# A causal attention layer with routed experts: queries and keys as two fp32r parts of 48 rows a head, two heads side by side in the rows of TensorE's array

## What is computed

```python
h = _layernorm(x, axis=-1) * (1 + ca) + sa
qkv = jnp.einsum('bsd,ed->bse', h, w_qkv) + b_qkv          # 16 heads of 16
scores = jnp.einsum('bhqd,bhkd->bhqk', q, k) / math.sqrt(Hd)
attn = jax.nn.softmax(scores + causal[None, None], axis=-1)
out = jnp.einsum('bhqk,bhkd->bhqd', attn, v)
x = x + ga * (jnp.einsum('bsd,ed->bse', out, w_out) + b_out)
h = _layernorm(x, axis=-1) * (1 + cb) + sb
x = x + gb * _L0_ffn_ref(h, ...)       # top-1 routing, 8 experts, gelu
```

## Time and profile before

| | us |
|---|---|
| median of 3 timed runs (785.0 to 790.39) | 787.31 |
| span of the profiled execution, first to last instruction | 782.6 |
| PE busy, share of the span | 689.1, 88% |
| DVE busy | 561.1, 72% |
| ACT busy | 459.5, 59% |
| POOL busy | 133.9, 17% |

### The profile page before, as it was taken

The page is one execution under the profiler, slowest core; times in us unless marked ns, Lnnn a source line. Parts: engine busy times, 40 slices in busy tenths (PEclk is TensorE's granted clock), DMA queues, the critical chain, the costliest instruction groups (busy, mean ns, idle before and its releaser), DMA issues.

```text
span 782.6 us, 12208 instructions
## 1 busy us (share of the span) xinstructions
PE 689.1 (88%) x4290; PEld 367.2 (47%) x4290; DVE 561.1 (72%) x1467; ACT 459.5 (59%) x962; POOL 133.9 (17%) x194
## 2 busy tenths in 40 slices
PE   4686989999999998999999999989996279999994
PEld 3564534432323343323332323242543269999994
DVE  7754778788888787988888898960435437777762
ACT  1422445566676667766677676657783336656551
POOL 6000222220001132003310201100105300121122
PEclk9869889999999999999999999999999559999998
DMA  7436126630006033005900006000004283455200
GB/s 243 109 76 144 41 57 147 162 68 14 2 0 162 1 81 81 2 1 124 308 1 1 1 1 214 1 28 1 28 28 162 90 234 115 155 182 201 92 23 17
DMA packets 42111, 66.53 MB, mean 85 GB/s; under 512 B 3822, under 2 KB 31985, under 8 KB 41466
## 3 DMA queue, kind: packets, MB, share of 16 engines
q1 hardware_dynamic: 39746, 59.44, 27.3%
q0 software_dynamic: 2304, 6.31, 2.2%
HBM read 39.36 MB, written 26.78 MB: 85 GB/s over the span
## 4 chain that ended last, share of the span: by engine, by line
PE 74%; DVE 10%; ACT 8%; issue 4%; DMA 2%; POOL 1%; SPq 0%; DVEq 0%; POOLq 0%; ACTq 0%
PE bank L1245 17%; PE bank L1295 15%; PE bank L1325 14%; PE bank L1430 9%; PE bank L1413 8%; ACT probs L802 4%; PE bank L1187 3%; DVE chunk_max L1049 2%; PE bank L1350 2%; PE bank L1216 1%; PE bank L1396 1%; ACT qk_sb L751 1%; PE bank L1373 1%; PE bank L1228 1%; DVE stats L907 1%
## 5 line engine op out<-in xcount | busy, mean ns | idle before, releaser
L802 ACT ACTIVATE probs<-bank 128x512 f32<-128x512 f32 (+3 forms) x640 | 298.3, 537 | 124.1 <-PE bank L1325 123.0
L1049 DVE TENSOR_REDUCE chunk_max<-bank 128x1 f32<-128x512 f32 x384 | 250.7, 685 | 36.9 <-PE bank L1295 35.9
L1325 PE MATMUL bank<-stacks 104*128 104x512 bf16 (+3 forms) x640 | 195.4, 356 | 13.5 <-ACT probs L802 10.1
L1295 PE MATMUL bank<-stacks 96*128 96x512 bf16 (+3 forms) x640 | 197.7, 359 | 7.9 <-DVE chunk_max L1049 3.2
L1245 PE MATMUL bank<-probs,v_sb 128*32 128x512 f32 (+3 forms) x1280 | 151.6, 546 | 0.1
L1055 DVE CUSTOM_DVE_ANT_0 masked<-bank,causal 128x128 bf16<-128x128 f32 (+3 forms) x256 | 120.7, 484 | 15.4 <-PE bank L1295 14.6
L1295 PEld LDWEIGHTS bank<-stacks 96*128 96x128 bf16 x640 | 56.0, 98 | 160.0 <-DVE chunk_max L1049 79.4
L698 POOL TENSOR_SCALAR_AFFINE_SELECT probs<-probs 128x512 f32<-128x512 f32 x64 | 40.6, 635 | 397.4 <-ACT probs L802 397.4
L1325 PEld LDWEIGHTS bank<-stacks 104*128 104x128 bf16 x640 | 62.2, 100 | 98.7 <-ACT probs L802 65.6
L1430 PE MATMUL bank<-w_split,acts 128*128 128x256 f32 x576 | 79.9, 284 | 0.0
L1430 PEld LDWEIGHTS bank<-w_split,acts 128*128 128x128 f32 x576 | 74.5, 190 | 1.5 <-issue 0.8
(11 more groups left out here) (140 smaller groups left out, 533.6 us busy)
## 6 DMA issues: line engine op xcount, KB each, us to landing
stacks<-qk_rows SPq DMA_DIRECT2D x6, 1536.0 KB, 12.4
w_raw<-w_in SPq DMA_DIRECT2D x8, 1024.0 KB, 5.0
w_raw<-w_down SPq DMA_DIRECT2D x8, 1024.0 KB, 8.0
qk_rows<-part SPq DMA_DIRECT2D x32, 192.0 KB, 2.9
slot_rows<-empty SPq DMA_DIRECT2D x1, 5140.0 KB, 28.9
slots_sb<-slot_rows SPq DMA_DIRECT2D x8, 514.0 KB, 4.0
qk_rows<-part SPq DMA_DIRECT2D x32, 128.0 KB, 2.4
stacks<-qk_rows SPq DMA_DIRECT2D x8, 384.0 KB, 4.5
```

The lines of the kernel that those rows point to most:

```text
L802: act.activation(probs[:, s % 3, h, 0:width], bank[SCORE_BANKS[u % 3]][:, 0:width], ACT.Exp)\
L1049: dve.tensor_reduce(to, src[:, 0:QB], AX.X, ALU.max).then_inc(max_read, 1)
L1295: pe.matmul(bank[MAX_BANKS[u % 3]][:, 0:width], stack(g, 0)[0:KR, h, q0:q0 + P], stack(g, 1)[0:KR, h, c * QB:c * QB + width], start=True, ...
L1325: pe.matmul(bank[SCORE_BANKS[u % 3]][:, 0:QB - lo], stack(g, 1)[0:KR + MR, h, kt * P:(kt + 1) * P], stack(g, 0)[0:KR + MR, h, b * QB + lo: ...
```

## The change

Queries and keys are split in two parts of type fp32r, three products, 48 rows a head. A head's stack then fits in half of the array's 128 rows: heads 0 and 1 of a group lie in rows 0 to 51, heads 2 and 3 in rows 64 to 115 (48 rows, and 4 for the maxima). The order of units within a query tile and of the heads in a step is such that neighbours in the list of max units, or of scores, come from different halves.

- ScalarE's second cast, one of two subtractions and the third part go; a store writes two parts in 4 DMAs instead of 6, a load reads in 4 DMAs (two halves, two sides) instead of 2. The bytes of a stack load are the same (half the rows, twice the width of a number).
- The maxima's rows no longer go to the stacks by ScalarE and VectorE: ScalarE copies the turned rows to `row_sb` (after.py L811), and SP sends them with two DMAs to both halves (L632). The ones go by eight DMAs out of `row_sb` (L599). `max_part` is fp32, and its transposes are fp32.
- SP now follows the plan: stores, loads (`load`), rows (`max_rows`), weights (`experts`) stand in one order. The fill of `slot_rows` follows group 3's load at once, as before.
- The planner's rates are others (a matmul at 3.4 columns a ns instead of 2.4, rows placed 3500 ns after their transposes instead of 1700), and the plan comes out differently.
- The values are kept 18 columns a head apart; a weigh matmul still loads 32.

```diff
-PARTS_Q = [0, 0, 0, 1, 1, 2]
-PARTS_K = [0, 1, 2, 0, 1, 0]
-KR = HD * len(PARTS_Q)
-MR = 2 * HG
+PAIRS = HG // 2
+HEADS = (0, 2, 1, 3)
+HALF = P // 2
+PARTS_Q = [0, 0, 1]
+PARTS_K = [1, 0, 0]
+NR = len(PARTS_Q)
+KR = HD * NR
+MR = 2 * PAIRS
...
-    return [[(qt, h, c) for qt in range(TB) for h in range(HG) for c in range(b + 1)] for b in range(NB)]
+    return [[(qt, 2 * a + p, c) for qt in range(TB) for p in range(PAIRS) for c in range(b + 1) for a in range(2)]
+            for b in range(NB)]
...
-TENSOR_RATE, VECTOR_RATE, SCALAR_RATE = 2.4, 0.96, 1.2
-VECTOR_FIXED, SCALAR_FIXED, MASK_TIME = 75, 60, 700
+TENSOR_RATE, VECTOR_RATE, SCALAR_RATE = 3.4, 0.96, 1.2
+VECTOR_FIXED, SCALAR_FIXED, MASK_TIME = 68, 50, 700
...
-            tensor(300, formed)
-            placed_at[n] = now + 1700
-            vector[-1] = max(vector[-1], now + 550) + 450
+            tensor(500, formed)
+            placed_at[n] = now + 3500
...
-        stacks = sb1("stacks", [P, 2, 2, HG, S], BF16)
+        stacks = sb1("stacks", [P, 2, 2, PAIRS, S], F32R)
...
+        def stack(g, side, h, rows):
+
+            return stacks[HALF * (h // 2):HALF * (h // 2) + rows, g % 2, side, h % 2, :]
...
+                if ev[0] == "load":
+                    g = ev[1]
+                    sp.wait_ge(parts_stored, 16 * STORES * NB * (g + 1))
+                    if g >= 2:
+
+                        sp.wait_ge(scored, HG * (last_step[(g - 1) * NB - 1] + 1))
+                    load_stacks(g, slice(0, S), stacked[g])
+                    if g == NG - 1:
+                        sp.wait_ge(empty_ready, 1)
+                        sp.dma_start(slot_rows.rearrange("(t p) d -> p t d", p=P),
...
+                if ev[0] == "max_rows":
+
+                    n = ev[1]
+                    g, b = divmod(n, NB)
+                    sp.wait_ge(misc_read_a, misc_reads(misc_use[ev])[0] + 1)
+                    for a in range(2):
+                        sp.dma_start(stacks[HALF * a + KR:HALF * a + KR + MR, g % 2, 0, :, b * QB:(b + 1) * QB]
+                                     .bitcast(F32),
+                                     row_sb[MR * a:MR * (a + 1), n % 2, :].bitcast(F32).rearrange("p (h s) -> p h s", h=1)
+                                     .broadcast_to([MR, PAIRS, QB])).then_inc(max_rows[n % 2], 16)
...
+        def low_part(eng, n, done):
+
+            eng.wait_ge(high_ready, n + 1)
+            eng.tensor_tensor(part[:, 1, :], qk_sb[:, :], part[:, 0, :].bitcast(F32), ALU.subtract).then_inc(done, 1)
...
-                if ev[0] == "split":
-                    second_part(ev[1], ev[2])
...
-                    rows = stack(g, 0)[KR:KR + MR, :, b * QB:(b + 1) * QB]
-                    dve.wait_ge(max_row0, n + 1)
-                    dve.tensor_copy(rows[:, 1:HG, :], rows[:, 0:1, :].broadcast_to([MR, HG - 1, QB]))\
-                        .then_inc(max_rows, 1)
...
-                    pe.matmul(bank[SCORE_BANKS[u % 3]][:, 0:QB - lo], stack(g, 1)[0:KR + MR, h, kt * P:(kt + 1) * P],
-                              stack(g, 0)[0:KR + MR, h, b * QB + lo:(b + 1) * QB], start=True, stop=True)\
+                    pe.matmul(bank[SCORE_BANKS[u % 3]][:, 0:QB - lo], stack(g, 1, head, KR + MR)[:, kt * P:(kt + 1) * P],
+                              stack(g, 0, head, KR + MR)[:, b * QB + lo:(b + 1) * QB], start=True, stop=True)\
```

More of the change, by code:

```diff
@@ L214, in project @@
                 parts_at[split[0]] = now + SPLIT_TIME
+        if loads and not split and loads[0] in parts_at and loads[0] - 2 in scored_at \
+                and now >= scored_at[loads[0] - 2] + 1000:
+            plan.append(("load", loads.pop(0)))
     weigh = None
```

241 lines of the change are left out of this document (118 added, 123 removed).

## The result

The changed kernel takes **947.7 us** (median of 4 runs, 946.79 to 949.98) against 788.17 of the kernel before (4 runs, 785.0 to 790.39): a ratio of 1.2035, with a 95% interval of 1.2001 to 1.2069. It was forecast at 759. The profiled execution spans 946.2 us (before 782.6), and its mean granted clock is 0.787 (before 0.943).

A forecast was written before the change was run, and what follows sets the result against it. PE was taken to bound the attention, VectorE next. Terms -41 + 15 + 5 - 7 + 2 - 2 = -28 us gave a span of 754.6 instead of 782.6, 759 us with the median's 4.7; range 715 to 794.

The forecast's parts named there:

- What bounds the kernel: Attention: PE bounds both its stages, at a granted clock of 0.98 in the first; VectorE is the next bound.
- stage B: The attention's two passes together, 80 to 510 us; PE busy 408.5 of 430 us, VectorE 367.3.
- the last sentence: Closing signs of being wrong, among them a fall of the granted clock in the attention's passes, with PE busy less.
- Part 1: Max and scores matmuls in the attention's passes: overlapping halves bring 0.179 down to 0.1435 us each, 41 us less.
- the 0.118 taken for them: Pace in us for a max or scores matmul following one in the other half, read from the experts' fp32r matmuls.
- Part 2: Scores moved ahead of the last max unit: 16 us less in the later stage, 16 more in the passes, 0.
- Parts 3 and 4: Maxima's rows sent by SP: later landing at blocks 0 to 3, 11, 15, +15; queue behind group 3's load, +5.
- the part on the queue: Block 10's rows wait behind group 3's load and fill, +5 us (0 to 15); group 2's load counted as covered.
- Part 5: Small things: VectorE's copies gone -7, fp32 transposes of the maxima +2, prologue -3 and +1 for the ones' DMAs.
- VectorE as the bound: Rival, chance 0.15: halves overlap better than counted, VectorE bounds the attention's passes, 716 us.
- that rival: Rival, chance 0.12: the halves don't overlap, matmul pace 0.179 or 0.190 us, 800 or 813 us.
- The rows' way: Rival, chance 0.13: row transfers wait behind SP's stores and more blocks are exposed, 25 us more, 784 us.

The follow-up runs named there:

- e6: Kernel before, max and scores matmuls reading only the first 48 rows of the bf16 stacks: 1091.1 us.
- e9: Kernel before, max and scores matmuls reading only the first 64 rows of the bf16 stacks: 907.4 us.
- e7: Kernel before, max and scores matmuls reading only the first 72 rows of the bf16 stacks: 781.9 us.
- e2: Changed kernel, max and scores matmuls reading 112 rows, both halves at once; maxima's rows sent to a scratch tile, waits kept: 848.4 us.
- e5: Kernel of e2, but nobody waits for the maxima's rows: 815.7 us.
- e10: Kernel of e6, but odd units take rows 64 to 104 (all scores; of max units those of groups 2 and 3): 890.8 us.
- e12: Kernel of e2, with the maxima's row transfers issued by ScalarE instead of SP: 862.9 us.
- e4: Changed kernel with heads and units ordered half by half, so fewer neighbours lie in different halves (396 instead of 745): 1043.5 us.
- e3: Kernel before with three waits of some 15 us put in on PE, before the first scores of blocks 2, 6 and 10: 835.7 us.
- e11: Kernel of e2, but max matmuls read 48 rows in alternating halves as in the changed kernel; scores keep 112 rows: 976.1 us.

## Why the prediction was wrong, step by step

**What bounds the kernel.** That PE bounds stage B was right, and stayed so. What the reading took for given was its clock: 0.98 in the earlier trace rows, as if it belonged to the chip and not to this stream of matmuls. That is the step that failed. In its place the runs show a clock that fell with the number of rows that the matmuls use: 0.641 with 48, 0.803 with 64, 0.947 with 72 (e6, e9, e7), and some 94 to 99 of the 160 us between before and after hang on it. The clock stood only in the last sentence as something that could go wrong, and with the wrong reason, that PE would be busy less. It fell at a wait, but it stayed down where PE was busy 30.00 of 30 us. The Trainium skill (TensorE: Matmul & The Clock Gate, What's actually happening) says that the gate is set "based on how busy the PE has been recently"; the busy time that a profile shows does not tell it here: 383.21 of 384 us busy at 1.2 GHz with 48 rows (e6), 2.4 GHz in most of the attention with 72 (e7).

**Part 1, forecast -41 us, bounds 0 to -70.** Apart from the clock, the mechanism was right and its size was off. At the full clock a max or scores matmul, over all widths, added 0.212 us instead of 0.221, 4% less (8 to 9% in the two stretches above, 0.198 and 0.201 instead of 0.218), where 20% was forecast (0.179 to 0.1435); on 1152 matmuls that is 10 to 23 us. Two pieces of the term were off. The type is not free: a 512-column fp32r matmul at full height adds 0.281 (e2), 13% over bf16, where "nothing is lost by type" was read from 256 columns in the experts. And neighbours in different halves don't run at the 0.118 taken for them: by the start times in the trace of the changed kernel, at the full clock, the next of two 512-column neighbours in different halves starts 0.194 us later on average (311 pairs, half of them within 0.121 us), in the same half 0.282 (72 pairs); without the pairs that have idle time between them it is 0.143 and 0.235. The prediction had named 0.2 us as a sign of being wrong. Many pairs start together, most of these 4 ns apart, but then the matmul behind them starts some 0.31 us later. The sign of the whole came from the clock: +99 us for the height.

**Part 2, forecast 0.** No run separates it.

**Parts 3 and 4, forecast +15 and +5, bounds 5 to 25 and 0 to 15.** Together +33 with the clock held up (e5 to e2), within the bounds and over the sum of 20. Block 15's way was as forecast, 0.58 + 0.64 + 2.22 us for 3.5, and the waits of blocks 1, 3, 11 and 15 in the changed kernel were 2.9 to 3.6 us, where 2 to 4 was forecast. Block 10's wait was 5.97 us for 5, by two misses that cancel: the rows landed 38 us after the load was issued instead of 32.5 (the fill took 37.0 us and not the 28.9 of the earlier trace rows), and TensorE came to them after 32 us instead of 27. Block 2's 14.2 us behind group 1's load were not foreseen at all; the part on the queue looked at the loads of groups 2 and 3 only. Without that wait, 14.1 us in e2, the others come to 19 us; that 33 still lies within the bounds is luck.

**Part 5, forecast -7, +2, -2.** VectorE's copies went, as said: it is busy 551.6 us instead of 561.1. It gained nothing, since VectorE had 129.1 us of idle time before its reductions over the whole span (36.9 in the stretch of the earlier trace rows). The maxima's transposes took 12.9 us instead of 6.4, at the lower clock. The ones, put at +1, cost some 5: TensorE's wait for block 0's rows is 8.0 us with them and 2.9 without (e2).

**The rivals.** VectorE as the bound needed a faster PE; in e10, at the full clock, VectorE comes level with it. The halves overlap, so that rival's mechanism is wrong, though its side was right. The rows' way cost 33 us and not the 45 it gave. No rival held the clock, and so the range ended at 794.

**A faster version** wasn't found. With nobody waiting and the clock up, the fp32r scheme stands at 815.7 us (e5), and the bf16 halves at 890.8 (e10); both leave out part of the layer, and both are above the kernel before.

## What to carry to other kernels

Before matmuls are made lower to fit two side by side, run the kernel as it is with fewer rows read: that one number would have shown that the clock falls (781.9 us with 72 rows, 907.4 with 64, 1091.1 with 48). Treat the granted clock of a stage as a result of that stage's matmuls, and price a change of their shape at both levels, not only at the one that the old profile shows. And keep a small transfer for which TensorE waits out of the time in which megabytes are on their way: look at every load, not only at the largest. Another queue alone took 14.1 us to 12.5 (e2, e12).

## What the runs showed of the hardware

- Bf16 matmuls with 48 rows in one half of the array ran at 1.2 GHz for 384 us on end, at 99.8% busy; with 64 rows the mean clock was 0.803, with 72 rows 0.947, with 96 and 104 rows 0.943. At 2.4 GHz what a 512-column matmul added didn't depend on the rows (0.250 us with 64, 0.247 with 72, 0.248 with 96 and 104).
- Taking the halves in turn more often raised the clock: 0.641 to 0.789 in bf16 (e6, e10), 0.692 to 0.787 in fp32r (e4, changed).
- Behind a wait of 14 to 15 us the clock was at 2.4 GHz again 4 to 7 us later with 96 and 104 rows (e3) and 4 us later with 112 (e2), while with 48 and 52 it stayed at 1.2 GHz for 97 us (changed). What ends such a stretch no run shows.
- A change between 48 and 112 rows from one matmul to the next cost 0.11 to 0.14 us (e11 against e2).
- More alternation of the halves, 745 neighbours instead of 396, was worth 11 to 15% of a 512-column fp32r matmul (e4, changed). The Trainium skill (TensorEngine Tiling (Array Packing), Theoretical Speedup) gives up to 2x for a contraction of at most 64; against full height in the same type, 0.281 us (e2), the traces show 1.3 in these stretches, with a weight load for each matmul.
- At the full clock an fp32r weight load took 184 ns with 48 rows (changed kernel, 274 to 341 us) and 188 with 112 (e5, 195 to 560 us); a bf16 one took 97 (before, 191 to 526 us).
